# Expert layers of a metaformer kernel without the warm products of zeros between the logits' turn and the scatter

## What is computed

```
x = x + L0_conv(ln_c(x))               # 2D spectral convolution, low modes only
t = tokens(x);  t = t + ffn(ln_t(t), L0 weights);  x = image(t)
x = x + L1_conv(ln_c(x))               # four sweeps over rows and columns, each step a 9-tap conv
t = tokens(x);  t = t + ffn(ln_t(t), L1 weights);  x = image(t)

def ffn(x, gate_w, gate_b, weight1, weight2):      # B=8 images, S=4096 tokens, D=32, E=16 experts, K=8
    logits = einsum('bsd,ed->bse', x, gate_w) + gate_b
    probs  = softmax(logits, axis=1)                # over the tokens
    topv, topi = top_k(probs, K) per image and expert
    pooled = sum over k of x[topi] * topv           # one row of 32 per image and expert
    h   = gelu([pooled, 1] @ weight1[e])            # 128 hidden units
    out = [h, 1] @ weight2[e]
    outputs[topi] += out * topv                     # scatter-add to the chosen tokens
```

## Time and profile before

| | us |
|---|---|
| median of 3 runs | 570.2 |
| lowest and highest | 566.84 and 570.34 |
| the profiled execution | 570.23 |
| its span, first to last instruction | 568.4 |

### The profile page before, as it was taken

One profiled execution on the slowest core, in us unless ns is written; L12 is line 12 of the kernel. 1 busy time (PEld: TensorE's weight loads), 2 busy tenths in 40 slices (PEclk: granted clock), 3 DMA queues, 4 the chain that ended last, 5 costly groups with the idle time before them and its releaser, 6 DMA issues.

```text
span 568.4 us, 25428 instructions
## 1 busy us (share of the span) xinstructions
PE 510.1 (90%) x11282; PEld 460.2 (81%) x11282; DVE 326.4 (57%) x767; ACT 275.3 (48%) x782; POOL 112.2 (20%) x240
## 2 busy tenths in 40 slices
PE   8978899887767999869999999889999999858897
PEld 8878899886656866759999999879999999757872
DVE  2757556754469438744554455435555455689736
ACT  4546455544585103644444444424445777658100
POOL 5000000000260000003333333643331044451000
PEclk9999999999999979979999999979999999977989
DMA  9940892051000000000000032420000244600007
GB/s 349 387 148 2 297 340 111 2 223 78 5 2 1 3 20 1 3 0 3 4 5 5 4 85 72 112 40 4 4 3 5 44 79 73 106 12 1 2 3 294
DMA packets 50260, 41.69 MB, mean 73 GB/s; under 512 B 44999, under 2 KB 45127, under 8 KB 48935
## 3 DMA queue, kind: packets, MB, share of 16 engines
q1 hardware_dynamic: 49304, 38.51, 21.1%
q0 software_dynamic: 704, 1.18, 1.0%
q10 hardware_dynamic: 144, 0.39, 0.2%
HBM read 27.49 MB, written 4.19 MB: 56 GB/s over the span
## 4 chain that ended last, share of the span: by engine, by line
PE 70%; DVE 15%; ACT 6%; DMA 3%; SPq 3%; issue 2%; POOL 1%; DVEq 0%; ACTq 0%
PE PS L786 38%; PE PS L755 5%; PE PS L562 5%; PE PS L544 3%; PE PS L705 3%; PE PS L506 2%; DMA RCD<-x_in 2%; PE PS L485 2%; SPq L341 2%; DVE RA L347 2%; PE PS L515 2%; DVE cand L1117 2%; DVE RCD L1122 2%; DVE sums L1083 1%; PE PS L448 1%
## 5 line engine op out<-in xcount | busy, mean ns | idle before, releaser
L786 PE MATMUL PS<-RE,conv_sb 128*64 128x64 f32 x6048 | 232.0, 232 | 4.6 <-DVE RE L1184 4.0
L786 PEld LDWEIGHTS PS<-RE,conv_sb 128*64 128x64 f32 x6048 | 217.3, 140 | 19.4 <-DVE RE L1184 4.8
L928 ACT COPY PS<-convb_sb 128x64 f32<-128x64 f32 x504 | 108.2, 215 | 114.1 <-DVE RE L1196 109.7
L1196 DVE SCALAR_TENSOR_TENSOR RE<-PS,RCD 128x64 f32<-128x64 f32 x252 | 56.6, 225 | 59.0 <-PE PS L786 59.0
L418 POOL COPY RCD<-RE 128x128 f32<-128x128 f32 x126 | 37.0, 294 | 157.2 <-DVE RE L1196 157.1
L1196 DVE SCALAR_TENSOR_TENSOR RE<-PS,RE 128x64 f32<-128x64 f32 x126 | 32.6, 259 | 28.6 <-PE PS L786 27.3
L1196 DVE SCALAR_TENSOR_TENSOR RE<-PS,RB 128x64 f32<-128x64 f32 x126 | 28.3, 225 | 28.1 <-PE PS L786 28.1
L562 PE MATMUL PS<-RE,RB 128*64 128x64 f32 x1024 | 32.9, 223 | 3.2 <-issue 1.7
L562 PEld LDWEIGHTS PS<-RE,RB 128*64 128x64 f32 x1024 | 31.3, 138 | 4.6 <-issue 3.7
L397 POOL TENSOR_TENSOR RE<-RA 128x1024 f32<-128x1024 f32 x3 | 5.7, 1892 | 148.6 <-ACT RA L899 148.6
L506 PE MATMUL PS<-warm 128*128 128x128 bf16 x418 | 29.6, 234 | 4.8 <-DVE warm L956 1.4
(11 more groups left out here) (117 smaller groups left out, 689.4 us busy)
## 6 DMA issues: line engine op xcount, KB each, us to landing
RE<-wspec SPq DMA_DIRECT2D x8, 2048.0 KB, 9.0
RA<-x_in SPq DMA_DIRECT2D x8, 512.0 KB, 7.6
RCD<-x_in SPq DMA_DIRECT2D x1, 4096.0 KB, 13.6
out<-RA SPq DMA_DIRECT2D x8, 512.0 KB, 2.7
RCD<-RB SPq DMA_DIRECT2D x58, 64.0 KB, 2.6
RE<-RCD SPq DMA_DIRECT2D x32, 80.0 KB, 2.6
conv_sb<-conv_w SPq DMA_DIRECT2D x1, 768.0 KB, 20.0
w_sb<-w SPq DMA_DIRECT2D x2, 264.0 KB
```

The source lines that it names most:

```text
L786: m = pe.matmul(conv_bank(s, u, c)[o:o + OC], conv_sb[:, s, d, o:o + OC], prev, start=False, stop=(d == 2), skip_group_check=True)
L928: act.copy(banks_of, convb_sb[:, s:s + 1].unsqueeze(2).to_broadcast([P, c1 - c0, n])).then_inc(s_seed, 1)
L1196: dve.scalar_tensor_tensor(out=state[:, state_slot(s, u), b0:b1, 1:1 + HO], in0=conv_bank(s, u, c), scalar=0.0, in1=row_at(SRC[s], s, q, u ...
```

## The change

Six of the calls of `keep_warm` in `experts` go, seven blocks of products as they run (the call with `if g < 2` runs twice): 180 products a layer, 360 in the kernel. Nothing else is touched: no wait, no transfer, no other instruction. 58 of the 418 warm products stay.

```diff
--- before.py
+++ after.py
@@ -690,7 +690,6 @@
                     group(G_LT[l] + g, [LT[:, 8 * g + n].rearrange("p h n -> p (h n)") for n in range(8)], None)
 
                 pe.wait_ge(s_ld, 4 * l + 4)
-                keep_warm(0, 110)
                 pe.wait_ge(s_rs, l + 1)
                 pe.transpose(PS[0:1, 6, 0:P], rsum[:, :], ident).then_inc(s_rt, 1)
 
@@ -714,15 +713,12 @@
                     for n in range(8):
                         m = pe.transpose(blk(banks(2 * (g % 2), 2), n), blk(E, 8 * g + n), ident)
                     m.then_inc(s_wt, 1)
-                    if g < 2:
-                        keep_warm(7, 14)
                     if g == 1:
                         pe.wait_ge(s_rr, l + 1)
                         pe.matmul(PS[0:C, 7, 0:P], ones[:, :], rs_row[:, :], start=True, stop=True).then_inc(s_rb, 1)
                     if g >= 1:
                         pool_tokens(g - 1)
                 pool_tokens(3).then_inc(s_pl, 1)
-                keep_warm(3, 16)
 
                 pe.wait_ge(s_pc, l + 1)
                 pe.wait_ge(s_w1[l], 16)
@@ -732,16 +728,13 @@
                         m = pe.matmul(PS[units, 6, B * e:B * e + B], w1_sb[:, e, units], pooled[:, :, e],
                                       start=True, stop=True)
                 m.then_inc(s_h, 1)
-                keep_warm(3, 8)
                 pe.wait_ge(s_g, l + 1)
                 for e in range(NE):
                     m = pe.matmul(PS[0:C, 7, B * e:B * e + B], w2_sb[:, l, e, :], hid[:, e, :], start=True, stop=True)
                 m.then_inc(s_o, 1)
-                keep_warm(3, 8)
                 pe.wait_ge(s_ob, l + 1)
                 pe.transpose(PS[:, 4, 0:C], eout[:, :, :].rearrange("p b e -> p (b e)"),
                              ident[0:C, 0:C]).then_inc(s_ot, 1)
-                keep_warm(3, 10)
 
                 pe.wait_ge(s_os, l + 1)
                 for k in range(16):
```

## The result

The changed kernel took 579.7 us (median of 576.9, 579.6, 579.9 and 625.0) against 568.5: a ratio of 1.0205, interval 1.0149 to 1.026. The execution at 625.0 had a mean granted clock of 0.73, where the other three had 0.92 to 0.93; no trace of it was kept, so where it lost its time isn't shown. The forecast was 573.4 us, no change over 1%. The time lies at the upper end of the range, where rival 1 with one layer was put (581).

The account below looks back on a forecast made before the run. In the expert layers the chain ran through TensorE and VectorE in turn. Clock losses less the zeros' gains gave +0.9 us in layer 0 and +2.25 in layer 1, +3.15 on 570.23: 573.4 us, range 567 to 580.

Parts of the forecast that it names:

- rival 1: Expert layers: clock stays at half through pooling; 581 us for one layer, 589 for both; 15 in 100.
- the forecast's own range: Whole kernel, clock falling in each layer and returning during transposes or early pooling: 569 to 579 us, 70 in 100.
- signs of being wrong: Full clock at first transposes, half clock to the scatter, or logits to scatter's start differing by over 3 us a layer.
- What is given back: Time gained by removing the zeros: 2.25 us in layer 0, 1.8 in layer 1, 4.05 in all.
- The fall: Without the 110, TensorE idles 8.25 us before the reciprocal; transposes at 181.86 certainly start at half clock.
- The return: Full clock 4.4 us after the transposes begin (bounds 2.6 and 6.2), losing 2.2 us a layer (1.3 to 3.1).
- its two ways: Half clock through pooling: pooling's 64 of 128 columns don't raise it, 12 in 100; or transposes don't restore it, 3.
- The rule of the Trainium skill: Transposes before pooling don't bring full clock back, since transpose-mode products don't engage it: 589 us; 3 in 100.
- Behind pooling: Expert products and scatter after pooling, both layers: earlier clock fall and half-clock losses, less the zeros' gains there.
- the two expert products: Behind pooling at half clock: first loses 0.4 us a layer; second 0.2 in layer 0, 0.5 in layer 1.
- the +0.95 of layer 1: Scatter, layer 1: half clock loses 2.2 us after the change against 1.25 before, so 0.95 more.
- the +0.35 of layer 0: Scatter, layer 0: half clock loses 2.2 us after the change against 1.85 before, so 0.35 more.

## Why the prediction was wrong, point by point

- *The number.* 579.7 lies just inside the range of 567 to 580, and that is luck: the forecast's own range ended at 579, and the rest came from part of rival 1. Two of the signs of being wrong that the prediction named showed in layer 1: half clock to the scatter, and a stretch from the reciprocal to the scatter 10.3 us longer, where 3 were allowed.
- *What is given back.* Right in place and size for the 14s: 1.4 us a layer were forecast, 1.3 show in a trace where the clock holds. The 110 stood before nothing, as the rows said, and were still the ones that counted: put back alone they undo nearly all of the loss, because with them the clock is full when the transposes start.
- *The fall.* Right: the clock is at half at the first transposes in every profile without the 110.
- *The return. This is the step that failed.* I took 4.4 us behind the start of the transposes, from 32 transposes that ran for 5.85 us without a break, and made a loss of 2.2 us of it, 1.3 to 3.1. But here 16 transposes run, for 3.68 us at half clock, and what follows them is of another kind. That was to be seen before: doubling the 0.86 us of a lot gives 3.4 us for two, less than the 4.4. In layer 0 the clock was back within 4 us (0.50 up to 183.30, 1.00 from 183.50) and the stretch cost 0.3 us net where 0.8 were forecast. In layer 1 it wasn't back by then, and 36 us were at half clock from the transposes on; pooling took 8.0 us more. The forecast took the return as a term with a size between two bounds; in the traces without the 110 and the 14s it came before pooling or as it began, 3 to 4.5 us behind the start of the transposes, or it missed at least half of pooling (only with wide products did it come within the first lot).
- *Rival 1* had the right price: 9.0 us net for a missed layer from the reciprocal to the first expert product, in a layer where the forecast had 1.2. Measured in layer 1 were 0.38 + 8.01 + about 1.5 for the first expert product (3.49 instead of 1.95) = 9.9. Of its two ways the first, pooling's narrow products, was the nearer one, but not by its reason, the 64 of 128 columns: with these kept and 64 columns moved instead of 32 only 2.2 us are lost. The 12 in 100 were far too few: the fastest execution of the changed kernel took 576.9. The rows didn't show this shape at half clock, and I let the resumed convolution, which moves 64 columns, stand for it.
- *The rule of the Trainium skill* ("TensorE: Matmul & The Clock Gate", Part 4, PE-mode transpose: full clock does not engage for transpose-mode products) fared no better behind the prediction: in layer 0 of the changed kernel the clock was back at 183.5, behind 3.7 us of transposes and the two small products that spread the row of reciprocals (L718, from 183.03). Its time, 589, missed the kernel by 9 us. Layer 1, where the same transposes didn't bring the clock back, doesn't speak against it, and whether these transposes run in the mode that the Trainium skill means, no row tells.
- *Behind pooling* I had +1.55 us in the two layers. The kernel without those zeros alone lost 3.3 (1.8 to 4.8). The terms that were too small are the two expert products. In that kernel's trace the first takes 3.46 and 2.58 us where it took 2.04 in each layer: 2.0 us lost, 0.8 forecast. The second takes 1.87 in both layers where it took 1.49 and 1.18: 1.1 us lost, 0.7 forecast. In the scatter of the changed kernel the +0.95 of layer 1 came out as +1.08, the +0.35 of layer 0 as -0.33.
- *The price of what I had forecast*, a fall and a return in time, is what the kernel with 64 moved columns shows: 1.0039, 2.2 us, where the forecast said 3.15.

What stays open: why the same transposes bring the clock back in one layer or execution and not in another; and why all eight executions of the changed kernel were slow, where without the 110 and the 14s only every second was. The zeros behind pooling, in which the two differ, stand behind the place where the clock misses; with so few executions, on different chips, chance or the chip may be all there is to it.

## What to carry to other kernels

Zeros that fill idle time can be worth more than those on the path: judge them by the clock at which the work behind them starts, and by whether that work can bring the clock back itself. Compare how long the work that could do so lasts with how long it took in the trace; if it is shorter or hardly longer, the cost can be the whole stage at half clock and not a ramp. A free size (here 32 or 64 moved columns at 2.06 and 2.08 us a lot) can decide it, as it seems to here.

## What the runs showed of the hardware that was not expected

- TensorE was busy for 33.0 of 37.4 us and had half clock all along (layer 1 of the changed kernel): with products of 64-column weights and 32 moved columns, and some transposes between, a busy engine wasn't enough there. With 64 moved columns no execution of twelve went over 572.3 us, and in the traced one the clock was full from the start of pooling or 0.3 us behind it.
- 16 transposes of 128x128 in 3.7 us were followed by full clock in one layer (changed kernel, layer 0, 183.5) and by half clock in the other (layer 1).
- At half clock a recorded instruction of pooling takes 55 ns (3.50 us for 64), at full clock 30 ns (1.95 us); at full clock a lot with 64 moved columns takes as long as one with 32 (2.08 and 2.06 us).
- A gap with 1.6 us of work in 3.2 us let the clock fall in one execution (the 110 put back, layer 1), in which the kernel took 576.1 us; the nine others took 565.7 to 568.6.
